# Early blocks 1 to 13 of a routed FFN kernel: the transposes of the next block's rows stand ahead of chunk 4 instead of chunk 2

## The reference

```
ys = y * scale
d = rsqrt(einsum('bi,io->bo', ys * ys, weight * weight) + EPS)
z = einsum('bsi,io->bso', x * ys[:, None, :], weight) * d[:, None, :]
logits = einsum('bsd,de->bse', z, Wr) + br
route_w = softmax(logits);  the two largest are kept and normalised -> routed
h = relu(einsum('bsd,edh->ebsh', z, W1) + b1)          # H = 1024
expert_out = einsum('ebsh,ehd->ebsd', h, W2) + b2
out = x + einsum('bse,ebsd->bsd', routed, expert_out)
```

## Time and profile before

| | us |
|---|---|
| time, median of 3 runs | 864.1 (863.81 to 865.29) |
| profiled execution, its own time | 864.32 |
| profiled execution, span on the core | 862.5 |
| PE busy | 839.0 (97%) |
| VectorE busy | 735.6 (85%) |
| ScalarE busy | 570.2 (66%) |
| GpSimd busy | 467.3 (54%) |
| mean granted TensorE clock | 0.995 |

### The profile page before, as it was taken

The page is one execution under the profiler, slowest core; times in us unless marked ns, Lnnn a source line. Parts: engine busy times, 40 slices in busy tenths (PEclk is TensorE's granted clock), DMA queues, the critical chain, the costliest instruction groups (busy, mean ns, idle before and its releaser), DMA issues.

```text
span 862.5 us, 19190 instructions
## 1 busy us (share of the span) xinstructions
PE 839.0 (97%) x5616; PEld 798.4 (93%) x5616; DVE 735.6 (85%) x1485; ACT 570.2 (66%) x1024; POOL 467.3 (54%) x424
## 2 busy tenths in 40 slices
PE   5998999999999999999999999999999999999996
PEld 5986999999999999999999999999999999999995
DVE  4796888899899879888888888888888888888884
ACT  6786665788787666556656665656565656688783
POOL 7983284545445344465546554655455545565553
PEclk9999999999999999999999999999999999999998
DMA  7894848776344454335432543253343524674772
GB/s 242 303 338 167 303 93 241 201 231 184 65 136 88 83 143 98 88 46 142 103 89 44 143 99 95 43 132 71 86 92 49 150 41 92 183 223 114 218 208 26
DMA packets 55002, 118.40 MB, mean 137 GB/s; under 512 B 7312, under 2 KB 33328, under 8 KB 54320
## 3 DMA queue, kind: packets, MB, share of 16 engines
q1 hardware_dynamic: 25040, 69.48, 23.9%
q0 software_dynamic: 25536, 35.69, 23.6%
q10 hardware_dynamic: 4384, 12.71, 4.3%
HBM read 91.07 MB, written 35.17 MB: 146 GB/s over the span
## 4 chain that ended last, share of the span: by engine, by line
PE 86%; DVE 7%; issue 2%; ACT 2%; DMA 1%; POOL 0%; ACTq 0%; DVEq 0%; SPq 0%; POOLq 0%
PE psum L1786 14%; PE psum L1770 14%; PE psum L1772 13%; PE psum L1771 13%; PE psum L1785 7%; PE psum L1787 5%; PE psum L1789 5%; PE psum L1788 5%; PE psum L1742 2%; PE psum L1783 2%; DVE w_parts L1469 2%; PE psum L1784 1%; PE psum L1652 1%; PE psum L1653 1%; DVE early_row_hot L1189 1%
## 5 line engine op out<-in xcount | busy, mean ns | idle before, releaser
L903 ACT ACTIVATE h<-psum,b_all 128x384 f32<-128x384 f32 (+1 forms) x376 | 208.6, 560 | 211.4 <-PE psum L1772 180.4
L1770 PE MATMUL psum<-z_hi,w_parts 128*128 128x384 f32 (+1 forms) x752 | 251.6, 335 | 3.4 <-DVE w_parts L1469 2.3
L1469 DVE TENSOR_TENSOR w_parts<-raw,w_parts 128x1024 fp32r<-128x1024 f32 x188 | 229.6, 1221 | 21.9 <-ACT w_parts L827 15.9
L1772 PE MATMUL psum<-z_hi,w_parts 128*128 128x384 f32 (+1 forms) x752 | 245.1, 326 | 0.0
L1771 PE MATMUL psum<-z_lo,w_parts 128*128 128x384 f32 (+1 forms) x752 | 245.1, 326 | 0.0
L1551 DVE TENSOR_TENSOR h_lo<-h,h_hi 128x384 fp32r<-128x384 f32 (+1 forms) x376 | 200.3, 533 | 29.4 <-ACT h L903 16.7
L827 ACT ACTIVATE w_parts<-raw 128x1024 fp32r<-128x1024 f32 x188 | 198.2, 1061 | 11.1 <-PE psum L1786 10.4
L687 POOL DMA_INDIRECT out<-y,idx_put x88 | 166.1, 1887 | 44.8 <-POOL idx_put L683 24.2
L1786 PE MATMUL psum<-w_parts,h_hi 128*128 128x512 f32 x525 | 188.6, 394 | 0.0
L1770 PEld LDWEIGHTS psum<-z_hi,w_parts 128*128 128x128 f32 x752 | 141.3, 188 | 9.6 <-ACT h L903 3.6
L1785 PE MATMUL psum<-w_parts,h_lo 128*128 128x256 f32 x525 | 146.6, 279 | 0.0
(11 more groups left out here) (256 smaller groups left out, 1154.3 us busy)
## 6 DMA issues: line engine op xcount, KB each, us to landing
raw<-in_experts SPq DMA_DIRECT2D x96, 512.0 KB
x_buf<-in_xT SPq DMA_DIRECT2D x12, 512.0 KB, 9.6
z_rows<-z_all ACTq DMA_DIRECT2D x2, 2112.0 KB
d_rep<-d_rows SPq DMA_DIRECT2D x3, 1056.0 KB, 6.7
z_rows<-z_all SPq DMA_DIRECT2D x1, 2112.0 KB, 13.2
z_rows<-z_once SPq DMA_DIRECT2D x1, 2112.0 KB, 15.2
raw<-in_xT SPq DMA_DIRECT2D x4, 512.0 KB, 8.8
z_row<-z_rows,idx_get POOLq DMA_INDIRECT x88
```

Source lines behind the costliest of these rows:

```text
L903: act.activation(h[c % NHP][:, 0:width], h_ps[c % n_h][:, 0:width], ACT.Relu, bias=b1_all[:, ds(e, 1), c]).then_inc(s_relu, 1)
L1469: dve.tensor_tensor(out=w_lo[k][:], in0=raw[k][:], in1=w_hi[k][:].bitcast(f32), op=ALU.subtract).then_inc(s_wlo, 1)
L1770: pe.matmul(hp, w1(w_hi, c, dc), z_hi[:, dc, 0:width], start=(dc == 0), stop=False)
L1772: ins = pe.matmul(hp, w1(w_lo, c, dc), z_hi[:, dc, 0:width], start=False, stop=(dc == DC - 1))
```

## The change

In `block_of_pe`, the condition that places the transposes among the chunks gave chunk 4 for block 0 (`fresh`), chunk 6 in tail blocks and chunk 2 in all others. Now it gives chunk 4 for all early blocks. Block 0 had it so already, the loop's blocks keep chunk 2, and so 13 blocks change.

```diff
                 lag = LAG_WIDE if tail or is_early(b) else LAG
                 for c in range(HC):
 
-                    if c == (4 if fresh else 6 if tail else 2) and not final:
+                    if c == (4 if is_early(b) else 6 if tail else 2) and not final:
                         transpose_z(b + 1, tail)
                     first_product(b, c, fresh, tail)
```

## The result

| | before | after |
|---|---|---|
| time, median of 6 runs, us | 864.55 | 867.93 |
| profiled execution, span, us | 862.5 | 866.0 |
| PE busy, us | 839.0 | 842.2 |

The ratio is 1.0038, with a 95% interval of 1.0027 to 1.0049: 3.4 us slower, between 2.3 and 4.2. A later comparison of the changed kernel with the kernel before gave 1.0039 (1.0025 to 1.0052).

The account below looks back on a forecast made before the run. TensorE, busy 97% of the span, was taken to bound the kernel. Eight blocks at 0.36 (2.9 us), blocks 7 and 11 (0.5) and blocks 6, 8, 10 (0) made 3.4 us: 867.5 from 864.1, range 865.7 to 869.1.

Parts of the forecast that it names:

- Step 1: Block 2, TensorE: chunk 2 can start at 115.40 and not 115.85, without stalling for the ReLU of chunk 0.
- Step 2: Block 2: chunk 3 waits from 116.44 to 116.71 for the ReLU of chunk 1, then takes 1.15 us, ending at 117.86.
- Step 3: Block 2, transposes and chunk 4: chunk 4 ends at 120.50, not 120.14; 0.36 us lost per block where nothing later waits.
- Step 4: ScalarE's queue: earlier chunks 2 and 3 bring their ReLUs no earlier; gain costed at nothing.
- Step 5: Blocks where VectorE holds TensorE up: waits absorb delay; loss 0 in 6, 8, 10, 0.31 in 7, 0.19 in 11.
- Step 6: Other things the transposes trigger (`s_zt`, GpSimd's gather, SyncE's transfers): cost 0, up to a slip of 4 us.
- A: Rival, chunk 3: the wait appears but its start-up is hidden by the weight load; 2.3 us more, 866.4; 7%.
- B: Rival, early blocks: the delay is given back everywhere later in the block; time 864.1; 8%.
- C: Rival, faster: chunk 3 need not wait and transposes fill waits at chunk 4; at most 0.5 us gained, 863.6; 3%.
- D: Rival, slower still: absorbing blocks don't absorb, as VectorE's chain shifts with TensorE; 4.7 us more, 868.8; 12%.
- E: Rival, order in the blocks: the change does not do what it says; no separate chance given.

Follow-up runs that it names:

- kernel before again: The kernel before, unaltered, built and profiled once more in the later comparison and timed against the kernel before: ratio 0.9995 (0.9986 to 1.0005).
- both pairs: Profiles of the kernel before and the changed kernel: the first ones (ratio 1.0038), then both unaltered once more (changed 1.0039, before 0.9995, against the kernel before).
- run with blocks 1 to 5 only: Against the kernel before, transposes moved from chunk 2 to ahead of chunk 4 in blocks 1 to 5 only, block 0 already so: ratio 1.0025 (1.0016 to 1.0034).

## Why the prediction was right

The forecast was 867.5 us from a median of 864.1, 3.4 us more; measured were 3.4 us (867.93 from 864.55).

Step 1, chunk 2 earlier without a stall: it started earlier by 0.45 to 0.47 us in the plain blocks. It was not quite free (1.11 us and not 1.04 in the run with transposes ahead of chunk 3), but in the changed kernel the wait behind it covers that.

Step 2, chunk 3 meets the ReLU of chunk 1: shown. Predicted were a start at 3.39 us and 1.15 us of duration; it was 3.40 and 1.16. Taking away the cast ahead of that ReLU took the wait away, and putting the transposes back in front of chunk 3 covered it. Block 0 was the piece of evidence that gave the size, and it held. That it could be read at all was luck: in the kernel before again block 0 ran partly at half the clock, and its wait at chunk 3 is not there.

Step 3, 0.36 us a block: 0.34 to 0.39 in the plain ones in both pairs. In block 3 it was 0.39 and 0.54; the second value starts at the ranks that stand ahead of chunk 2 there, and was not followed up.

Step 4, no gain from the earlier chunks 2 and 3: ScalarE's next rows came as far into the block as before (bias copies 3.24 us in, in both kernels).

Step 5, the absorbing blocks: predicted for 6, 7, 8, 10 and 11 were 0, 0.31, 0, 0 and 0.19. The first pair gave -0.01, -0.02, -0.19, +0.09 and +0.22, the second -0.19, +0.36, -0.55, -0.06 and +0.19. The sum of the five was 0.5 predicted, 0.1 and -0.25 measured, and the mechanism is there: in block 10 chunk 4 ends 0.36 us late and chunk 6 starts 0.17 and 0.01 late. The -0.19 of block 6 and the +0.09 of block 10 are VectorE's cast of two lengths (last section) and not the move. But for block 8 I read a wait of 0.71 us as a property of the block. It belongs to the late start in block 7, which only some profiles have. Without it the price of block 8 is 0.25. The changed kernel was never run where the late start is absent. My estimate for it there, from the lengths, is 3.9 us over blocks 1 to 13: 0.36 for each of the seven plain blocks and for block 7, 0.4 for blocks 3 and 11, 0.25 for block 8. With the late start in both kernels it was 3.1 and 2.8.

That the sum met the measured 3.4 us to the tenth is therefore partly luck. This term was too large by 0.4 us and block 14 gave back 0.1, which nobody had counted; against them stand 0.4 us ahead of block 0, where the kernels are the same, and 0.1 us more in the eight blocks that lose in full.

Step 6, no new delay through `s_zt`: moving the transposes as far as chunk 6 cost 4.7 us, and the plain blocks' 0.38 to 0.48 us leave no room for more. No wait of TensorE for gathered rows appeared among the early blocks.

The rivals. A, start-up hidden: fell, chunk 3 took 1.16 us in block 2, and the first matmul behind the wait shows 0.45 where a plain one shows 0.34. The list of waits of the weight loads shows 13 loads held for L903, so the load waits with its matmul: both start at 117.48 in block 2. The Trainium skill, "TensorE: Matmul & The Clock Gate", section "Part 2: What happens when you issue a matmul", has loads pulled ahead of matmuls in flight; the trace agrees where nothing is waited for (load at 118.96, matmul at 119.07), and past a wait it did not happen. B, given back everywhere: fell in the seven plain blocks. C, faster: fell with the ReLU's end at 3.35 us. (The border of 3.17 us that it names should be 3.07 by its own numbers, arrival at 3.12 less 0.05; nothing hangs on it.) D, absorbed nowhere: fell by block 6 in every run, and by block 8 in the pair that was compared. E: the transposes stand where the order says.

## What to carry to other kernels

Before moving a small piece of work on the busiest engine, look at what becomes ready while it runs: its neighbour may be in time only because of it. An instruction that costs 0.46 us and covers a wait of 0.27 costs 0.36 more in another place, and one place later (chunk 3) would have kept most of the cover. The block that already has the other order (here block 0) gives the price; a wait that seems able to absorb a delay should be seen in more than one profile, and on more than one chip, before it is counted on.

## What the runs showed of the hardware

The waits of chunk 3 on TensorE cost their length and 0.11 us of start-up (1.15 or 1.16 us and not 1.04). The first weight load, which is 0.11 us ahead of its matmul elsewhere, waited too and started with it. The wait of chunk 2, which ended just in time, still cost 0.07 us, by my reading through that load.

Block 0 took 17.77 to 17.80 us where TensorE had the full clock and 18.96 to 18.99 where a stretch of it ran at half. The same program, the kernel before, had both.

VectorE's cast of chunk 1 in block 6 takes 0.64 us in some profiles and 0.37 in others, of the same program too (the changed kernel has 0.63 and, again, 0.37), beside a GpSimd `DMA_INDIRECT` (L677) of 1.81 or 1.62 us. Timelines of the kernel before again, VectorE:

```profile
185.89 0.36 DVE L1548 CAST h_hi<-h 128x384 fp32r<-128x384 f32 x1
186.28 0.56 DVE L1551 TENSOR_TENSOR h_lo<-h,h_hi 128x384 fp32r<-128x384 f32 x1
186.76 0.64 DVE L1548 CAST h_hi<-h 128x384 fp32r<-128x384 f32 x1
```

and of the run with blocks 1 to 5 only:

```profile
189.09 0.43 DVE L1548 CAST h_hi<-h 128x384 fp32r<-128x384 f32 x1
189.56 0.56 DVE L1551 TENSOR_TENSOR h_lo<-h,h_hi 128x384 fp32r<-128x384 f32 x1
190.03 0.37 DVE L1548 CAST h_hi<-h 128x384 fp32r<-128x384 f32 x1
```

The two casts start 2.62 and 3.5 us into the block in both. The pair that begins with 0.36 goes on with 0.64 and makes the block 0.17 us longer. A contest of VectorE and GpSimd over something shared would look like this, but no run was made to show it.
